# Recurrence step of an sLSTM decoder layer: nine VectorE operations become eight, with two gates' tanh in one ScalarE instruction and an exponential computed twice

## What is computed

```python
def step(carry, wx_t):
    h, c, n, m = carry
    raw = wx_t + jnp.einsum('bhd,hdgo->bhgo', h, rk) + b
    ir, fr, zr, og = (raw[:, :, 0], raw[:, :, 1], raw[:, :, 2], raw[:, :, 3])
    lfm = m + jax.nn.log_sigmoid(fr)
    mn = jnp.maximum(ir, lfm)
    ig = jnp.exp(ir - mn)
    fg = jnp.exp(lfm - mn)
    cn = fg * c + ig * jnp.tanh(zr)
    nn = fg * n + ig
    hn = jax.nn.sigmoid(og) * cn / nn
    return ((hn, cn, nn, mn), hn)
```

## Time and profile before

| what | us |
|---|---|
| median of 3 runs | 4346.27 |
| lowest and highest of them | 4340.91, 4349.16 |
| the profiled execution, its own time | 4332.73 |
| span of its trace | 4331.0 |
| PE, DVE, ACT busy in the span | 3704.3, 3573.7, 2871.1 |

### The profile page before, as it was taken

One profiled execution on the slowest core, in us unless ns is written; L12 is line 12 of the kernel. 1 busy time (PEld: TensorE's weight loads), 2 busy tenths in 40 slices (PEclk: granted clock), 3 DMA queues, 4 the chain that ended last, 5 costly groups with the idle time before them and its releaser, 6 DMA issues. The chain is left out here.

```text
span 4331.0 us, 114618 instructions
## 1 busy us (share of the span) xinstructions
PE 3704.3 (86%) x42154; PEld 2228.9 (51%) x42154; DVE 3573.7 (83%) x16163; ACT 2871.1 (66%) x9230; POOL 1036.1 (24%) x1217
## 2 busy tenths in 40 slices
PE   5777777747899999999989999999868999999987
PEld 3433433434555555555555555555534555555555
DVE  7887888778888888888888888888758888888875
ACT  4565566545666666666666666666736888888884
POOL 1000000000000000000000000000006888889983
PEclk6555555556999999999999999999978999999998
DMA  3222222211333333343333333334343223322300
GB/s 100 69 68 71 67 71 71 71 20 25 82 77 81 74 75 80 66 93 74 73 82 78 78 74 79 76 66 91 81 93 90 50 69 79 79 63 56 79 25 25
DMA packets 262094, 305.41 MB, mean 71 GB/s; under 512 B 21752, under 2 KB 255032, under 8 KB 256376
## 3 DMA queue, kind: packets, MB, share of 16 engines
q1 hardware_dynamic: 258356, 293.73, 28.4%
q10 hardware_dynamic: 3176, 4.36, 0.4%
HBM read 241.03 MB, written 55.78 MB: 69 GB/s over the span
## 5 line engine op out<-in xcount | busy, mean ns | idle before, releaser
L1364 PEld LDWEIGHTS G<-st,rec_w 128*128 128x128 f16 x19456 | 609.4, 100 | 849.5 <-DVE st L1553 810.2
L1364 PE MATMUL G<-st,rec_w 128*128 128x1 f16 x19456 | 685.3, 165 | 309.6 <-DVE st L1553 296.9
L1825 POOL TENSOR_TENSOR plt<-pft,pht 128x512 f16<-128x512 f32 x765 | 866.6, 1165 | 155.2 <-DVE pht L2068 85.0
L1314 PE MATMUL OA<-pf,vals 128*97 128x512 f32 (+1 forms) x1632 | 881.6, 623 | 0.8
L1225 ACT ACTIVATE st<-hb 32x16 f16<-32x16 f32 x1216 | 260.9, 215 | 654.3 <-DVE hb L1548 653.2
L152 DVE TENSOR_REDUCE mx<-MB 128x1 f32<-128x512 f32 (+1 forms) x832 | 536.3, 661 | 56.8 <-PE MB L144 49.4
L1205 ACT ACTIVATE pf<-SC,ln_prob 128x512 f32<-128x512 f32 (+1 forms) x816 | 562.3, 689 | 20.6
L152 DVE TENSOR_REDUCE mx<-MT 128x1 f32<-128x512 f32 (+1 forms) x832 | 523.7, 665 | 53.0 <-PE MT L1874 42.8
L1820 ACT ACTIVATE pft<-ST,ln_prob 128x512 f32<-128x512 f32 (+1 forms) x816 | 538.6, 691 | 34.3 <-PE ST L1896 33.9
L1818 ACT ACTIVATE pht<-ST,ln_prob 128x512 f16<-128x512 f32 x510 | 352.5, 691 | 193.6 <-PE ST L1896 188.5
L135 PE MATMUL SC<-q_in,k_in 65*128 65x128 f16 (+1 forms) x3264 | 480.6, 224 | 0.0
(11 more groups left out here) (365 smaller groups left out, 7178.2 us busy)
## 6 DMA issues: line engine op xcount, KB each, us to landing
kc_in<-scr_k SPq DMA_DIRECT2D x384, 256.0 KB, 4.3
k_in<-scr_k SPq DMA_DIRECT2D x192, 256.0 KB, 4.9
vc<-scr_v SPq DMA_DIRECT2D x16, 1644.8 KB, 15.4
kc<-scr_k SPq DMA_DIRECT2D x32, 816.0 KB, 12.9
scr_v<-v_hl SPq DMA_DIRECT2D x24, 1032.0 KB, 5.7
scr_k<-k_hl SPq DMA_DIRECT2D x192, 128.0 KB, 1.7
k<-scr_k SPq DMA_DIRECT2D x16, 816.0 KB, 6.5
kc_in<-scr_k SPq DMA_DIRECT2D x32, 192.0 KB, 3.7
```

What stands on the lines that cost most here:

```text
L1314: pe.matmul(OA[0:at.DC + 1, :], at.vals[0:rows, i, :], pf[0:rows, tile % 2, :], start=(i == 0), stop=(i == KT - 1)).then_inc(pv_done, 1)
L1364: mm = pe.matmul(g[:, t, c:c + 1], rec_w[:, c, :], st[:, c:c + 1], start=False, stop=(c == C - 1), skip_group_check=True)
L1825: return eng.tensor_tensor(pl[0:k, t % NP_, :], pf[0:k, t % NP_, :], ph[0:k, t % NP_, :], ALU.subtract)
```

## The change

ScalarE still runs four instructions a step, on other tiles. The gates stand in `G` in another order (set by the table `GATE_AT`: forget in partitions 0 to 31, cell in 32 to 63, input in 64 to 95, output in 96 to 127), so that one tanh on 64 partitions gives both tf and tz (`tfz`). The exponential of the input gate is computed twice: into partitions 32 to 63 (`e_beside_z`), beside tz, and into `added[:, 1]` in partitions 0 to 31, beside the product that goes to `added[:, 0]`. VectorE then adds numerator and denominator in one instruction, and the output gate is multiplied by the numerator (`oc`) instead of the reciprocal.

```diff
+GATE_AT = (2, 0, 1, 3)
...
-                            s.activation(tf[:, :], g[Q:2 * Q, t, :], ACT.Tanh, scale=1.0 / G_SCALE).then_inc(f_ready, 1)
-                            s.activation(ei[:, :], g[0:Q, t, :], ACT.Exp, scale=1.0 / G_SCALE).then_inc(i_and_u, 1)
-                            s.activation(tz[:, :], g[2 * Q:3 * Q, t, :], ACT.Tanh, scale=1.0 / G_SCALE).then_inc(z_ready, 1)
-                            s.activation(to[:, :], g[3 * Q:P, t, :], ACT.Tanh,
-                                         scale=1.0 / G_SCALE).then_inc(o_and_r if t < CH - 1 else o_last, 1)
+                            s.activation(tfz[:, :], g[0:2 * Q, t, :], ACT.Tanh, scale=1.0 / G_SCALE).then_inc(f_ready, 1)
+                            s.activation(e_beside_z[Q:2 * Q, :], g[2 * Q:3 * Q, t, :], ACT.Exp, scale=1.0 / G_SCALE).then_inc(e_ready, 1)
+                            s.activation(added[:, 1, :], g[2 * Q:3 * Q, t, :], ACT.Exp, scale=1.0 / G_SCALE).then_inc(i_u_v, 1)
+                            s.activation(to[:, :], g[3 * Q:P, t, :], ACT.Tanh, scale=1.0 / G_SCALE).then_inc(o_ready, 1)
...
-                            v.scalar_tensor_tensor(out=uu[:, :, :], in0=tf[:, :].unsqueeze(1).broadcast_to([Q, 2, C]),
-                                                   scalar=1.0, in1=cn[:, :, :], op0=ALU.add, op1=ALU.mult).then_inc(i_and_u, 1)
-                            dve.wait_ge(i_and_u, 2 * n)
-                            v.scalar_tensor_tensor(out=cn[:, 1, :], in0=ei[:, :], scalar=E_TOP, in1=uu[:, 1, :],
-                                                   op0=ALU.min, op1=ALU.add).then_inc(n_ready, 1)
-                            dve.wait_ge(n_ready, n)
-                            v.reciprocal(rn[:, :], cn[:, 1, :]).then_inc(o_and_r, 1)
-                            dve.wait_ge(z_ready, n)
-                            v.scalar_tensor_tensor(out=vv[:, :], in0=ei[:, :], scalar=E_TOP, in1=tz[:, :],
-                                                   op0=ALU.min, op1=ALU.mult).then_inc(v_ready, 1)
+                            v.scalar_tensor_tensor(out=uu[:, :, :], in0=tfz[0:Q, :].unsqueeze(1).broadcast_to([Q, 2, C]),
+                                                   scalar=1.0, in1=cn[:, :, :], op0=ALU.add, op1=ALU.mult).then_inc(i_u_v, 1)
+                            dve.wait_ge(e_ready, n)
+                            v.scalar_tensor_tensor(out=added[:, 0, :], in0=e_beside_z[Q:2 * Q, :], scalar=E_TOP, in1=tfz[Q:2 * Q, :],
+                                                   op0=ALU.min, op1=ALU.mult).then_inc(i_u_v, 1)
+                            dve.wait_ge(i_u_v, 3 * n)
+                            v.scalar_tensor_tensor(out=cn[:, :, :], in0=added[:, :, :], scalar=E_TOP, in1=uu[:, :, :],
+                                                   op0=ALU.min, op1=ALU.add).then_inc(cn_ready, 1)
+                            dve.wait_ge(cn_ready, n)
+                            v.reciprocal(rn[:, :], cn[:, 1, :]).then_inc(r_and_oc, 1)
+                            dve.wait_ge(o_ready, n)
                             if t < CH - 1:
-                                dve.wait_ge(o_and_r, 2 * n)
-                                v.scalar_tensor_tensor(out=ww[:, :], in0=to[:, :], scalar=1.0, in1=rn[:, :],
-                                                       op0=ALU.add, op1=ALU.mult).then_inc(w_and_c, 1)
+                                v.scalar_tensor_tensor(out=oc[:, :], in0=to[:, :], scalar=1.0, in1=cn[:, 0, :],
+                                                       op0=ALU.add, op1=ALU.mult).then_inc(r_and_oc, 1)
...
-                            dve.wait_ge(v_ready, n)
-                            v.tensor_tensor(cn[:, 0, :], uu[:, 0, :], vv[:, :], ALU.add).then_inc(w_and_c, 1)
-                            dve.wait_ge(w_and_c, 2 * n)
-                            v.scalar_tensor_tensor(out=now[:, t, :], in0=ww[:, :], scalar=0.5 * H_SCALE, in1=cn[:, 0, :],
+                            dve.wait_ge(r_and_oc, 2 * n)
+                            v.scalar_tensor_tensor(out=now[:, t, :], in0=rn[:, :], scalar=0.5 * H_SCALE, in1=oc[:, :],
                                                    op0=ALU.mult, op1=ALU.mult).then_inc(h_ready, 1)
```

More of the change, by code:

```diff
@@ L502, in slstm_stage @@
         gt = sb("gt", [HALF_UP, 2, P])
-        tf = sb("tf", [Q, C])
-        ei = sb("ei", [Q, C])
-        tz = sb("tz", [Q, C])
+        tfz = sb("tfz", [2 * Q, C])
+        e_beside_z = sb("e_beside_z", [2 * Q, C])
+        added = sb("added", [Q, 2, C])
         to = sb("to", [Q, C])
         uu = sb("uu", [Q, 2, C])
-        vv = sb("vv", [Q, C])
         rn = sb("rn", [Q, C])
-        ww = sb("ww", [Q, C])
+        oc = sb("oc", [Q, C])
         ok = sb("ok", [Q, C])
@@ L701, in _ @@
                     dve.wait_ge(z_time, 3)
-                    v.tensor_copy(gate_b[3 * Q:P, 0, :], time_w[3 * Q:P, :])
+                    v.tensor_copy(gate_b[3 * Q:P, GATE_AT[0], :], time_w[3 * Q:P, :])
                     dve.wait_ge(z_sel, 1)
@@ L705, in _ @@
                         rows = slice(j * Q, (j + 1) * Q)
-                        v.tensor_scalar(shift_w[rows, 0:Q], ident[rows, rows], part, None, ALU.mult)
+                        v.tensor_scalar(shift_w[rows, GATE_AT[0] * Q:(GATE_AT[0] + 1) * Q], ident[rows, rows], part, None, ALU.mult)
                     dve.wait_ge(d_ln, 32)
@@ L718, in _ @@
                                 if g < 2:
-                                    ins = v.tensor_scalar(gate_w[0:2 * Q, l, 2 * pair:2 * pair + 2, g, :], from_w,
+                                    ins = v.tensor_scalar(gate_w[0:2 * Q, l, 2 * pair:2 * pair + 2, GATE_AT[g], :], from_w,
                                                           part * G_SCALE, None, ALU.mult)
                                 else:
-                                    ins = v.tensor_scalar(gate_w[2 * Q:P, l, 2 * pair:2 * pair + 2, g, :], from_w, part,
+                                    ins = v.tensor_scalar(gate_w[2 * Q:P, l, 2 * pair:2 * pair + 2, GATE_AT[g], :], from_w, part,
                                                           ln1_g[d, l:l + 1], ALU.mult, ALU.mult)
@@ L729, in _ @@
                     dve.wait_ge(z_rc, 1)
-                    v.tensor_copy(rec_w[0:3 * Q, :, :], rcmb[:, :, :, :].rearrange("p c g o -> p c (g o)")).then_inc(z_hi, 1)
+                    for g, row in enumerate(GATE_AT):
+                        ins = v.tensor_copy(rec_w[0:3 * Q, :, row * Q:(row + 1) * Q], rcmb[:, :, g, :])
+                    ins.then_inc(z_hi, 1)
                     dve.wait_ge(z_hi, 1)
-                    v.tensor_tensor(rec_w[2 * Q:3 * Q, :, :],
-                                    rcmb[2 * Q:3 * Q, :, :, :].rearrange("p c g o -> p c (g o)"),
-                                    rec_w[2 * Q:3 * Q, :, :], ALU.subtract)
+                    for g, row in enumerate(GATE_AT):
+                        low = rec_w[2 * Q:3 * Q, :, row * Q:(row + 1) * Q]
+                        v.tensor_tensor(low, rcmb[2 * Q:3 * Q, :, g, :], low, ALU.subtract)
                     dve.wait_ge(d_wk, 16)
@@ L749, in _ @@
                     for g, part in enumerate(GATE_PART):
-                        ins = v.tensor_scalar(bias[:, g, :], bnat[:, g, :], part * B_SCALE, None, ALU.mult)
+                        ins = v.tensor_scalar(bias[:, GATE_AT[g], :], bnat[:, g, :], part * B_SCALE, None, ALU.mult)
                     ins.then_inc(z_b, 1)
@@ L769, in slstm_stage @@
         OA = ps("OA", [P, 512])
[L771 to L774, removed]
+        pre_ready, f_ready, e_ready, i_u_v, o_ready = (
+            sem(n) for n in ("pre_ready", "f_ready", "e_ready", "i_u_v", "o_ready"))
+        cn_ready, ok_ready, r_and_oc, renewed = (
+            sem(n) for n in ("cn_ready", "ok_ready", "r_and_oc", "renewed"))
         h_ready, h_high, parts_ready, k_ready, s_ready = (
@@ L1545, in _ @@
-                            dve.wait_ge(v_ready, n)
-                            v.tensor_tensor(cn[:, 0, :], uu[:, 0, :], vv[:, :], ALU.add).then_inc(w_and_c, 1)
-                            dve.wait_ge(w_and_c, 2 * n)
-                            v.scalar_tensor_tensor(out=now[:, t, :], in0=ww[:, :], scalar=0.5 * H_SCALE, in1=cn[:, 0, :],
+                                                       op0=ALU.add, op1=ALU.mult).then_inc(ok_ready, 1)
+                                dve.wait_ge(ok_ready, p + 1)
@@ L1549, in _ @@
+                                v.tensor_tensor(oc[:, :], ok[:, :], cn[:, 0, :], ALU.mult).then_inc(r_and_oc, 1)
+                            dve.wait_ge(r_and_oc, 2 * n)
+                            v.scalar_tensor_tensor(out=now[:, t, :], in0=rn[:, :], scalar=0.5 * H_SCALE, in1=oc[:, :],
                                                    op0=ALU.mult, op1=ALU.mult).then_inc(h_ready, 1)
-                            v.scalar_tensor_tensor(out=st[0:Q, :], in0=ww[:, :], scalar=0.5 * H_SCALE, in1=cn[:, 0, :],
+                            v.scalar_tensor_tensor(out=st[0:Q, :], in0=rn[:, :], scalar=0.5 * H_SCALE, in1=oc[:, :],
```

4 lines of the change are left out of this document (removed).

## The result

| what | before | after |
|---|---|---|
| median of 4 runs, us | 4347.72 | 4291.28 |
| lowest and highest, us | 4340.91, 15313.67 | 4288.04, 4294.32 |
| the profiled execution, us | 4332.73 | 4289.60 |
| mean granted clock of TensorE | 0.856 | 0.857 |

The change makes the kernel faster: the ratio of the times is 0.9875, with an interval of 0.9856 to 0.9895. One run of before, at 15313.67 us, was disturbed and is left out of the ratio; the other three have a median of 4346.27 and lie between 4340.91 and 4349.16, and against them the change is worth 55 us. The forecast was 4303 with a range of 4273 to 4322.

A forecast was written before the change was run, and what follows sets the result against it. PE waits for VectorE's dependent chain in 908 recurrence steps; 45 us gained there, less 1 for last steps and 1 for setup, takes 43 off 4332.7, so 4290 profiled and a median of 4303, range 4273 to 4322.

The forecast's parts named there:

- What bounds the kernel: In the recurrence, PE's weight load waits for VectorE's last instruction in 908 steps; VectorE's own dependences set `uu` to `hb`.
- The second rival: Recurrence: PE eats part of the gain, only 534 of the 908 steps gain, 27 us less 2, 4321; chance 0.11.
- a sign of being wrong: In the new profile: all VectorE distances as foretold, but fewer waits of PE for DVE and more steps with PE late.
- The held product: VectorE's product `added[:, 0]` reads another partition group, so it starts only 0.03 us after `uu` ends, in every step.
- The first rival: The product is not held and starts 0.08 us before `uu` ends: 33 us more gain, 4270; chance 0.12.
- `oc` beside the reciprocal: On VectorE `oc` takes `vv`'s place, starting 0.17 us after the reciprocal's start and lasting 0.10 us.
- The fourth rival: `oc` is held until the reciprocal is done; `hb` comes 0.11 us later than before, 100 us slower, 4446; chance 0.03.
- The sum: `uu` to `hb` takes 0.91 us instead of 0.96: 908 steps x 0.05 us = 45 us, 43 after two losses.
- The last step of a chunk: There the new `ok` and `oc` wait for one another, taking back the gain in 38 steps, 2 us at most.
- its gates stay where they were: ScalarE's first exp stays at 601.12, the second takes the place of `tz`, and `to` stays at 601.52.
- The setup: The two instructions writing `rec_w` become four pieces each, costing 0.5 us at the least or 1.5; 1 taken.
- VectorE's busy time: To fall by some 158 us, as 0.57 us of instructions become 0.44, 1216 times, while the span falls by only 43.

The follow-up runs named there:

- the run with the gates far: The changed kernel with the gates reordered in G so that the wide tanh reads from partitions 64 to 127: 4306.23 us, ratio 0.9919.
- the spare one: The changed kernel with a ninth, independent VectorE instruction between `oc` and `hb` in every step: 4294.79 us, ratio 0.9887.
- the same eight in another order: The changed kernel with the output gate multiplied by the reciprocal again, after it, still eight VectorE operations: 4538.89 us, ratio 1.0453.
- two runs: Changed kernel, wide tanh reading partitions 64 to 127: 4306.23 us; kernel before, forget gate moved to partitions 0 to 31: 4324.61 us, ratio 0.9963.
- the repeat: The changed kernel unaltered, timed again against the kernel before: 4288.06 us, ratio 0.9879.

## Why the prediction was right, by its own steps

**What bounds the kernel** held: PE waits for DVE in about three quarters of the steps, and a saving between `uu` and `hb` comes through in these. The second rival (only 534 of them gain) is not borne out: 534 x 0.04 less 2 would be 19 us, and the DVE part measured 35, 30 to 41 by the interval (the run with the gates far). That is 908 x 0.039, the whole 0.04 of the timeline in every step of the chain. The prediction had named fewer waits of PE for DVE as a sign of being wrong; they did fall, from 908 to 884, but 24 x 0.04 is 1 us.

**The held product** was the main choice, and right. The first rival took away the hold and gave 33 us more; the run with the product reading from partition 0 measured 45. Its mechanism was sized with half of 600 x 0.11, and the 600 came from a wrong reading: the earlier trace rows count only the waits that left VectorE idle, and 1216 less these, 801, was taken for the late steps. In the trace of before `uu` follows 0.03 us behind the end of `tf` in 698 steps, so 518 come late. In the run itself `hb` came 0.11 us earlier in the 257 latest steps and 0.07 in 289 others by the medians; three quarters of that sum are 35 us, and what makes the other 10 of the 45 is open. The count of instructions says nothing here: one more is free (the spare one), while the same eight in another order cost 251 us.

**`oc` beside the reciprocal** was right to the hundredth, 0.17 behind its start and 0.10 long. The fourth rival, an `oc` held by its partitions, did not come about, and no run makes it so. The run that undoes `oc` puts it behind the reciprocal by a real dependence: `hb` 0.24 us later than in the changed kernel and 0.20 later than before, where the rival had 0.11 later than before.

**The sum** put 0.05 us a step; it measured 0.04, so the term of 45 us is 35 to 37. Where it lost 0.01: the forecast laid every start at the end before it plus 0.03, with ends rounded to hundredths. The rows have `cn` at 0.41, the reciprocal at 0.62, `oc` at 0.79 and `hb` at 0.92 where the forecast had 0.40, 0.61, 0.78 and 0.91. In steps that wait for tanh its 0.91 was 0.015 short and its 0.96 for before 0.005; in late steps 0.91 was 0.005 short and 0.96 was 0.004 long. The last step of a chunk was to lose its gain and lost 0.04 us more, at most 3 us in place of 2.

**A term was missing**, and it has the larger effect: ScalarE's first gate starts before the end of the instruction ahead of it, worth 16 to 18 us by two runs. The prediction said of ACT that its gates stay where they were, and looked at which partitions VectorE reads but not at which ACT reads. The two errors have opposite signs: 36 + 17 - 1 - 1 = 51 us where the forecast had 43, and the repeat measured 52. So a part of the agreement is luck. The forecast of 4303 is 12 us above the measured 4291, since the medians are 55 apart. 8 of these 12 are the difference of the terms; the other 4 lie between 51 and 55, with a median of three runs on the side of before that spread over 8 us. That the profiled executions differ by just the foretold 43 is chance: that of before lay 13.5 us under its median, that of after only 1.7.

**The setup**: the four pieces of each `rec_w` write take 1.43 and 2.49 us, where the earlier trace rows have 1.22 and 2.28.

```profile
26.59 1.43 DVE L731 CAST rec_w<-rnat 96x512 f16<-96x512 f32 x4
28.05 2.49 DVE L736 TENSOR_TENSOR rec_w<-rnat,rec_w 32x512 f16<-32x512 f32 x4
```

That is 0.4 us together, at the lower bound of 0.5; the first product of the recurrence comes 0.6 us later than before, and 0.2 later in the changed kernel's second run. The rate of the first was not lost.

**VectorE's busy time** fell by 3573.7 - 3497.4 = 76 us, not the 158 foretold. That figure added the durations of instructions that overlap, and busy time counts a moment once. By the earlier trace rows, `cn`, then the 0.03 us that `vv` lasts beyond the reciprocal, then `ww` and `cn` together from 601.81 to 602.05 make 0.16 + 0.03 + 0.24 = 0.43 us; now it is 0.16 + 0.18 + 0.03 = 0.37. The difference, 0.06 x 1216, is 73.

## What to carry to other kernels

Lay a dependent chain of short instructions out on the clock of a real step, with starts, ends and the partitions that each reads; the longest path through it is the price, and the count of instructions is not. Where an order of gates, heads or chunks in the partitions is free, let the instruction that starts a chain behind other work read from the group that this work has read from (here 0), on ScalarE as well as on VectorE. An arrangement that wins where an engine waits can cost time where it comes late: a version may be chosen step by step from the trace, and this gave another 26 us.

## What the runs showed of the hardware

On ScalarE a gate that read from partition 0 started 0.03 to 0.10 us before the end of a 128-partition activation that also read from 0, and a gate that read from partition 32 or 64 started 0.02 to 0.03 after it. Reading from partition 0 is not enough by itself. In the kernel before, line 980 reads `TP` in PSUM from 0, behind `to`, which has read `G` from 96, and in all 38 steps where it stands there it starts 0.02 us after the end:

```profile
1500.16 0.18 ACT L1219 ACTIVATE to<-G 32x16 f32<-32x16 f32 x1
...
1500.36 0.38 ACT L980 ACTIVATE gt<-TP 84x256 f32<-84x256 f32 x1
```

Line 877, which reads SBUF from 0, starts 0.09 us before the end of the same `to`, in 38 steps too. So partition 0 itself is ruled out, and the group that was last read from PSUM fits all of these. Nor is the same group in PSUM always enough: `added` reads the group that `e_beside_z` has read, but writes to another, and starts 0.02 us after its end in all 1216 steps. That it is the written group that holds it there was not tried. The gates behind the first start 0.20 us apart in every kernel, whatever they read; only behind an early first gate is it less at times, 0.18 at the least.

The tanh on 64 partitions lasts 177 ns (180 where it reads from partition 64), and that on 32 lasted 176. The forecast had allowed up to 0.02 us more.

A VectorE instruction with two waits, the second of them on its predecessor, started 0.10 us (by the median of 1178 steps) after that one's end instead of 0.03, with a semaphore instruction between them. This is one place in one kernel, and no run takes the second wait away alone.
